# Linear attention's odd units normalised by GpSimd and turned by VectorE through 32x32 squares in memory, even units turned by TensorE

## The chip, the cores and the metric

The kernel runs on one core of a Trainium2 chip. The time is the device time in microseconds (us) of one execution. The engines of the core are TensorE (PE), VectorE (DVE), ScalarE (ACT), GpSimd (POOL) and SyncE (SP), which issues nearly all transfers. They run independently and meet at semaphores.

## What is computed

The input is x of shape (16, 56, 56, 128) in float32. Layer 0 is a group norm and window attention (7x7 windows, shifted by 3), with a residual. Then, with t of shape (16, 3136, 128):

```
t = t + linear_attention(layernorm(t))   # this stage is changed
t = t + recurrence(layernorm(t))

def linear_attention(x):                 # per image, causal
    q, k, v = split(x @ W.T + b)
    q = elu(q) + 1;  k = elu(k) + 1
    num[t] = q[t] @ cumsum(outer(k, v))[t]
    den[t] = q[t] . cumsum(k)[t] + 1e-6
    return num / den

def recurrence(x):                       # batch norm of x @ W.T, then
    y = sigmoid(wx[t] + y @ V.T)         # one step per token
```

## The kernel before

There are three stages in one program: window attention (128 window rows of 392 tokens, pipelined steps n), linear attention, and the scan of the recurrence. The middle one is changed. `pipeline` runs the window stage's steps on each engine and calls the next step of the linear stage inside them from a step `join` on; when the window stage is over, the linear steps run alone. `join` is derived from `JOIN` (125) with an offset for each engine: SyncE `JOIN - 3`, GpSimd `JOIN + 1`, the others `JOIN`.

The linear stage has 196 units of 256 tokens, each two chunks `a` of 128 tokens. Its steps are numbered -4 to 204. Every engine has an order of work written by hand for step n, and each piece waits for semaphores that count units:

- SyncE loads the tokens of unit n+4 into `xc` (L780), and stores finished rows of unit n-5 with their statistics into the table `t2`, in `pieces` that don't cross a 196-token segment (L789). Buffers: 8.
- VectorE measures unit n+3 and the finished unit n-4 (`measure`, L1118, and `aggregate`, L1130), combines queries and keys of unit n (`combine`, L1085), takes denominators, normalises unit n+2 (`normalise`, L1071 for the first four, then L1074), computes the output tokens of unit n-3 (`attend`, L1145) and masks the scores (`inner_out`, L1095).
- GpSimd adds epsilon and takes the root of the variances (`statistics`, L1019 and L1025), and copies 1/std into the table's rows (`remember`, L1030).
- TensorE turns the normalised tokens of unit n+1 (`turn_tokens`, L825) into PSUM, multiplies with the weights (`queries_and_keys`, L835, `values`, L847), turns the keys (L857), forms scores (L870), the outer products (L886), numerators (L904, L908) and second moments (L921).
- ScalarE copies the turned tokens to `uT` and adds 1 (`turned_out`, L951), takes exponentials (L958), evicts values, keys and states, and scales the finished tokens (L993).

The order on TensorE in step n is:

```python
queries_and_keys(n)
turn_keys(n - 1)
turn_tokens(n + 1)
outer(n - 2, 0)
numerators(n - 3)
moments(n - 8)
outer(n - 2, 1)
values(n + 1)
scores(n)
```

In the window stage, the pieces that share the queues with the first linear steps are: GpSimd lowers the scores by their peak (L618), normalises the next unit (L611), weighs the probabilities by 1/sum (L625) and adds the bias to the residual tokens; from `JOIN` on the linear step is run ahead of the weighing. TensorE turns the weighed probabilities (L333). VectorE adds the residual (L455) into `y`, which has four buffers. SyncE loads residual tokens (L223) and stores `y` (L232) to `x1`, from which the linear stage loads.

## Time and profile before

| | us |
|---|---|
| median of 3 runs | 1789.76 (1787.34 to 1792.07) |
| profiled execution | 1784.76 |
| its span in the trace | 1782.8 |
| TensorE busy in the span | 1749.7 |
| VectorE busy | 1509.8 |
| ScalarE busy | 1269.8 |
| GpSimd busy | 1073.7 |

The linear stage's matmuls with the query and key weights start at 771.1 us and end at 1555.5; the window stage lies before, the scan behind. All figures of the profile are from the one profiled execution. Matmul rows overlap each other, so their distance from start to start counts, not their duration. TensorE's granted clock is 1.00 of its full speed in all stages shown but a few microseconds at the seams.

### The profile page before, as it was taken

The numbers are of one execution on the slowest core, as the hardware profiler recorded it, in microseconds if no ns is written. First come the engines' busy times: TensorE is split into PE (matmuls) and PEld (weight loads), VectorE is DVE, ScalarE is ACT, GpSimd is POOL, SyncE is SP. The second block draws the span as 40 slices with busy tenths as digits, with TensorE's granted clock in tenths as the row PEclk, the third lists the DMA queues.
The fourth block names the chain that finished last, engine by engine and source line by source line (L and its number), as shares of the span: only waits on it lengthen the run. The fifth ranks groups of instructions, "written<-read, shape, count | busy, mean of one in ns | idle before, by whom it ended". The sixth has DMA issues, their size and how long they took to land.

```text
span 1782.8 us, 58142 instructions
## 1 busy us (share of the span) xinstructions
PE 1749.7 (98%) x19648; PEld 1587.7 (89%) x19648; DVE 1509.8 (85%) x4546; ACT 1269.8 (71%) x3387; POOL 1073.7 (60%) x1202
## 2 busy tenths in 40 slices
PE   7999999999999999989999999999999999989997
PEld 6888888888888888879999999999999999989997
DVE  7889888888888888778888888888888888868787
ACT  5877778887887788856666666666666666657776
POOL 6887888888888888843333333333333333368874
PEclk9999999999999999999999999999999999999999
DMA  5333343433333332313334434343434443457774
GB/s 167 105 103 104 104 110 99 109 107 102 110 103 104 106 106 70 83 43 70 73 67 68 70 68 70 68 67 68 70 68 70 68 68 70 86 178 277 291 278 176
DMA packets 361816, 188.30 MB, mean 106 GB/s; under 512 B 221760, under 2 KB 348720, under 8 KB 356656
## 3 DMA queue, kind: packets, MB, share of 16 engines
q1 hardware_dynamic: 360368, 183.40, 41.0%
q8 instruction: 164, 2.69, 0.7%
q14 instruction: 132, 1.08, 0.2%
q10 hardware_dynamic: 1152, 1.13, 0.2%
HBM read 106.58 MB, written 77.87 MB: 103 GB/s over the span
## 4 chain that ended last, share of the span: by engine, by line
PE 52%; issue 28%; POOL 17%; DVE 1%; DMA 1%; POOLq 0%; ACT 0%; ACTq 0%; SPq 0%; DVEq 0%
POOL la_rstd L1025 12%; PE k_psum L349 7%; PE k_psum L299 6%; PE k_psum L292 6%; PE k_psum L1488 6%; PE k_psum L317 6%; PE k_psum L333 6%; PE k_psum L365 5%; PE k_psum L1478 5%; PE k_psum L283 5%; POOL la_spread L1019 3%; POOL la_tn L1030 2%; DMA wa_group<-in_group 0%; POOLq L42 0%; DMA t<-la_tn 0%
## 5 line engine op out<-in xcount | busy, mean ns | idle before, releaser
L1019 POOL TENSOR_SCALAR la_spread<-la_mv 128x4 f32<-128x4 f32 (+1 forms) x203 | 46.2, 228 | 476.1 <-DVE la_mv L1130 476.0
L618 POOL TENSOR_TENSOR wa_prob<-wa_prob,wa_peak 128x784 f32<-128x784 f32 x128 | 195.0, 1523 | 116.8 <-DVE wa_peak L484 116.8
L966 ACT ACTIVATE la_ve<-k_psum 128x256 f32<-128x256 f32 x196 | 75.6, 386 | 231.9 <-PE k_psum L847 231.9
L1025 POOL TENSOR_TENSOR la_rstd<-la_spread,k_exponent 128x4 f32<-128x4 f32 (+1 forms) x203 | 207.8, 1024 | 17.2 <-POOL la_spread L1019 0.4
L625 POOL TENSOR_TENSOR wa_prob<-wa_prob,wa_inv 128x784 f32<-128x784 f32 x128 | 195.2, 1525 | 11.3 <-DVE wa_inv L445 11.3
L835 PE MATMUL k_psum<-la_uT,la_wt 128*128 128x256 f32 x784 | 201.9, 380 | 0.0
L1085 DVE SCALAR_TENSOR_TENSOR la_fqk<-k_psum,la_raised 128x512 f32<-128x512 f32 x196 | 135.4, 691 | 72.8 <-ACT la_raised L958 72.6
L1562 ACT ACTIVATE sc_y<-k_psum,sc_cols 128x128 f32<-128x128 f32 x414 | 152.3, 368 | 51.9 <-PE k_psum L1488 8.8
L476 DVE TENSOR_TENSOR wa_prob<-k_psum,wa_bias 128x784 f32<-128x784 f32 x128 | 124.9, 976 | 66.2 <-PE k_psum L317 66.1
L1488 PE MATMUL k_psum<-sc_y,sc_vT 128*128 128x128 f32 x824 | 171.0, 289 | 0.0
L958 ACT ACTIVATE la_raised<-k_psum,la_minus_one 128x512 f32<-128x512 f32 x196 | 134.8, 688 | 43.9 <-PE k_psum L835 43.7
L1478 PE MATMUL k_psum<-sc_uT,sc_fT 128*128 128x128 f32 x832 | 161.7, 276 | 2.8 <-DVE sc_uT L1503 2.8
L525 ACT ACTIVATE wa_kb<-k_psum,wa_own 128x392 f32<-128x392 f32 x256 | 136.5, 584 | 38.2 <-PE k_psum L292 38.2
L544 ACT ACTIVATE wa_vb<-k_psum 49x256 f32<-49x256 f32 x256 | 97.0, 379 | 90.8 <-PE k_psum L299 89.1
L333 PEld LDWEIGHTS k_psum<-k_ident,wa_prob 113*128 113x128 f32 x1024 | 118.2, 142 | 43.5 <-issue 23.7
L886 PE MATMUL k_psum<-la_ve,la_kt 128*128 128x129 f32 (+1 forms) x768 | 150.7, 278 | 1.8 <-ACT la_state L982 1.6
L904 PE MATMUL k_psum<-la_ve,la_aT 128*128 128x129 f32 x784 | 151.7, 276 | 0.0
L908 PE MATMUL k_psum<-la_state,la_fqk 128*128 128x129 f32 (+1 forms) x768 | 148.9, 275 | 0.0
L637 POOL TENSOR_TENSOR wa_xb<-wa_xw,wa_bout 112x384 f32<-112x384 f32 (+1 forms) x128 | 146.9, 1148 | 0.0
L349 PE MATMUL k_psum<-wa_pT,wa_vb 128*64 128x49 f32 x4096 | 146.5, 224 | 0.1
L556 ACT ACTIVATE wa_pT<-k_psum 128x452 f32<-128x452 f32 x256 | 140.2, 548 | 8.4 <-PE k_psum L333 5.3
L349 PEld LDWEIGHTS k_psum<-wa_pT,wa_vb 128*64 128x64 f32 x4096 | 130.0, 138 | 17.8 <-ACT wa_pT L556 0.5
(137 smaller groups left out, 5205.3 us busy)
## 6 DMA issues: line engine op xcount, KB each, us to landing
la_xc<-x SPq DMA_DIRECT2D x196, 128.0 KB, 3.0
wa_xT<-in_x_cm SPq DMA_DIRECT2D x124, 196.0 KB, 3.3
sc_tb<-t SPq DMA_DIRECT2D x17, 1320.0 KB, 8.3
out<-sc_ob SPq DMA_DIRECT2D x17, 1280.0 KB, 5.4
wa_xw<-in_x_tok SPq DMA_DIRECT2D x64, 224.0 KB, 2.7
wa_xw<-in_x_tok SPq DMA_DIRECT2D x64, 168.0 KB, 2.3
x<-wa_y SPq DMA_DIRECT2D x64, 168.0 KB, 2.8
x<-wa_y SPq DMA_DIRECT2D x48, 224.0 KB, 2.9
```

What stands on the lines that cost most here:

```text
L333: mm = nc.tensor.transpose(b_pt[:, q * LANES:(q + 1) * LANES], prob[0:LANES, k % S, hp, 2 * h + p].rearrange("p j c -> p (j c)"), ident[0: ...
L349: mm = nc.tensor.matmul(b_ot[64 * hp:64 * hp + 64, c:c + WIN], vb[:, k % S, h * 2 + w // 2, w % 2, hp].rearrange("p a b -> p (a b)"), pT[: ...
L618: nc.gpsimd.tensor_tensor(s, s, peak[:, k % S, :].unsqueeze(2).broadcast_to([128, PAIRS * HEADS, WIN]), ALU.subtract).then_inc(lowered, 1)
L625: nc.gpsimd.tensor_tensor(s, s, inv[:, k % S, :].unsqueeze(2).broadcast_to([128, PAIRS * HEADS, WIN]), ALU.mult).then_inc(weighted, 1)
L835: mm = nc.tensor.matmul(b_qk[:, j * 2 * P:(j + 1) * 2 * P], wt[:, j * C:(j + 1) * C], uT[:, n % S, :], start=True, stop=True)
L886: nc.tensor.matmul(b_kv[:, 0:E], kt[part, n % S, a, :], ve[part, n % S, a, :], start=fresh, stop=True, skip_group_check=True).then_inc(kv_ ...
L904: mm = nc.tensor.matmul(held[:, a * E:(a + 1) * E], aT[:, n % S, a, :], ve[:, n % S, a, :], start=True, stop=begins(c), skip_group_check=True)
L908: mm = nc.tensor.matmul(held[0:p, a * E:(a + 1) * E], fqk[:, n % S, 0, a * P:a * P + p], state[:, c % S, :], start=False, stop=True, skip_ ...
L1025: nc.gpsimd.tensor_tensor(rstd[:, n % S, used], spread[:, used], exponent[:, used], ALU.pow).then_inc(rooted, 1)
L1478: nc.tensor.matmul(b_state[h][t % 2][:, 0:HALF], ffn.fT[:, :], uT[:, t // 2 % U_PAIRS, t % 2, half(h)], start=True, stop=False).then_inc(w ...
L1488: nc.tensor.matmul(b_state[h][t % 2][:, 0:HALF], ffn.vT[:, :], before, start=False, stop=True).then_inc(v_done[h], 1)
L1562: nc.scalar.activation(ffn.state(t)[:, half(h)], b_state[h][t % 2][:, 0:HALF], ACT.Sigmoid, bias=ffn.shift_bn).then_inc(y_made[h], 1)
```

## The change

Units are treated by parity. Even units go as before, with tiles of their own (`ue`, two buffers). Odd units are normalised by GpSimd (one `tensor_scalar` a chunk, with 1/std and a shift `1 - mean/std` that GpSimd computes, so that the added 1 is in it) into `uo`, which holds two odd units, laid out in quads of 32 channels. Every four units SyncE stores `uo` to the tensor `squares` in memory and loads it back in four pieces into `us`, so that each 32x32 square lies where its transpose is wanted but for the turn inside the square. VectorE turns the squares of one unit with one transpose instruction straight into `uT`. TensorE's turns and ScalarE's eviction remain for even units only.

What moves with it: the loads of tokens run ten units ahead instead of four (14 buffers instead of 8), measuring and roots eight instead of three, `AHEAD` is 12 instead of 7, so that finished units are measured at the same step as before; the linear steps begin at -10 instead of -4 and `JOIN` is `NU - 9` (119) instead of `NU - 3`. The raised values have two buffers instead of four. The table's rows of a chunk are stored with one transfer, without `pieces`.

```diff
-        JOIN = NU - 3
+        JOIN = NU - 9
...
-        XS = 8
-        AHEAD = 7
+        XS = 8
+        XC = 14
+        NS = 10
+        RS = 2
+        AHEAD = 12
...
+        shift = sb("shift", [P, 2])
+        ue = sb("ue", [P, 2, 2, C])
+        uo = sb("uo", [P, QUADS, 4, SQ])
+        us = sb("us", [128, QUADS, 4, SQ])
...
+        def table_rows(c):
+
+            first, block = c * P, SQ * STEPS
+            return bass.AP(t2.tensor, (first % block * NB + first // block) * SF, [[NB * SF, P], [block * NB * SF, QUADS], [1, SF]])
...
-        steps = range(-4, UNITS + 9)
+        def await_tokens(eng, n):
+
+            eng.wait_ge(odd_turned if n % 2 else even_out, n // 2 + 1)
+
+        steps = range(-10, UNITS + 9)
...
+                def store_normed(n):
+
+                    if not inside(n, UNITS) or n % 4 != 3:
+                        return
+                    sp.wait_ge(odd_normed, n // 2 + 1)
+                    sp.dma_start(squares[n // 4], uo[:, :, :, :].rearrange("p q a r -> p q (a r)")).then_inc(uo_stored, 16)
+
+                def load_squares(n):
+
+                    if not inside(n, UNITS) or n % 4 != 1:
+                        return
+                    sp.wait_ge(uo_stored, (n // 4 + 1) * 16)
+                    at_least(sp, odd_turned, n // 2)
+                    for q in range(QUADS):
+                        sp.dma_start(us[q * SQ:(q + 1) * SQ].rearrange("p k a r -> p k (a r)"),
+                                     squares[n // 4, :, q, :].rearrange("(k p) r -> p k r", p=SQ)).then_inc(us_loaded, 16)
...
-                    for a, p, q, col, s in pieces(n):
-                        dst = bass.AP(t2.tensor, ((col % SQ * STEPS + s) * NB + col // SQ) * SF,
-                                      [[NB * SF, q - p], [SQ * STEPS * NB * SF, QUADS], [1, SF]])
-                        sp.dma_start(dst, tn[p:q, n % XS, a]).then_inc(stored[n % XS], 16)
+                    for a in range(2):
+                        sp.dma_start(table_rows(2 * n + a), tn[:, n % XS, a]).then_inc(stored[n % XS], 16)
...
-                    load(n + 4)
+                    load(n + 10)
+                    load_squares(n + 3)
                     store(n - 5)
+                    store_normed(n + 7)
...
                 def turn_tokens(n):
-                    if not inside(n, UNITS):
+
+                    if not inside(n, UNITS) or n % 2:
                         return
...
                 def turned_out(n):
-                    if not inside(n, UNITS):
-                        return
-                    act.wait_ge(u_turned, n + 1)
+                    if not inside(n, UNITS) or n % 2:
+                        return
+                    act.wait_ge(even_turned, n // 2 + 1)
...
+                def place_shift(n):
+
+                    if not inside(n, UNITS) or n % 2 == 0:
+                        return
+                    pool.wait_ge(rooted, n + 1)
+                    at_least(pool, odd_normed, n // 2)
+                    nc.gpsimd.tensor_tensor(shift[:, :], mv[:, n % NS, 0, :, 0], rstd[:, n % NS, 0:2], ALU.mult).then_inc(lowered, 1)
+                    pool.wait_ge(lowered, n // 2 + 1)
+                    nc.gpsimd.tensor_scalar(shift[:, :], shift[:, :], -1.0, 1.0, ALU.mult, ALU.add).then_inc(shifted, 1)
+
+                def normalise(n):
+
+                    if not inside(n, UNITS) or n % 2 == 0:
+                        return
+                    pool.wait_ge(shifted, n // 2 + 1)
+                    at_least(pool, uo_stored, n // 4 * 16)
+                    for a in range(2):
+                        last = nc.gpsimd.tensor_scalar(uo[:, :, n % 4 // 2 * 2 + a, :], quads(xc[:, n % XC, a, :]), rstd[:, n % NS, a:a + 1],
+                                                       shift[:, a:a + 1], ALU.mult, ALU.add)
+                    last.then_inc(odd_normed, 1)
...
-                    statistics(n + 3)
-                    remember(n + 3 - AHEAD)
+                    place_shift(n + 7)
+                    normalise(n + 7)
+                    statistics(n + 8)
+                    remember(n + 8 - AHEAD)
...
+                def turn_tokens(n):
+
+                    if not inside(n, UNITS) or n % 2 == 0:
+                        return
+                    dve.wait_ge(us_loaded, (n // 4 + 1) * 16 * QUADS)
+                    at_least(dve, qk_ready, n - S + 1)
+                    at_least(dve, v_ready, n - S + 1)
+                    nc.vector.transpose(uT[:, n % S, :], us[:, :, n % 4 // 2 * 2:n % 4 // 2 * 2 + 2].rearrange("p k a r -> p a k r")).then_inc(odd_turned, 1)
...
-                    measure(n + 3)
+                    measure(n + 8)
                     combine(n)
                     denominators(n - 3)
                     invert(n - 3)
                     normalise(n + 2)
-                    aggregate(n + 3)
+                    turn_tokens(n + 2)
+                    aggregate(n + 8)
                     attend(n - 3)
                     inner_out(n)
```

## Rows read from the trace of the kernel before

**Rows 1.** Stages: busy us (instructions) of PE, PEld, DVE, ACT, POOL; clock; DMA; GB/s.

```profile
400.00:600.00 200.00, 200.00 (x3117) 167.74 (x3116) 177.44 (x299) 160.20 (x376) 166.47 (x147) 1.00 0.39 106
...
760.00:800.00 40.00, 34.09 (x309) 29.60 (x306) 27.95 (x97) 19.71 (x57) 17.10 (x23) 0.96 0.16 39
...
1100.00:1200.00 100.00, 100.00 (x799) 95.66 (x799) 86.08 (x402) 65.67 (x200) 36.52 (x75) 1.00 0.40 68
```

**Rows 2.** Timeline of TensorE in the linear stage: start us, us, engine, line.

```profile
1101.95 1.03 PE L835 MATMUL k_psum<-la_uT,la_wt 128*128 128x256 f32 x4
...
1103.03 0.38 PE L825 MATMUL k_psum<-k_ident,la_u 128*128 128x128 f32 x2
...
1103.25 0.39 PE L886 MATMUL k_psum<-la_ve,la_kt 128*128 128x129 f32 x2
...
1105.93 1.03 PE L835 MATMUL k_psum<-la_uT,la_wt 128*128 128x256 f32 x4
```

**Rows 3.** Timeline of VectorE and GpSimd in the same stretch.

```profile
1103.73 0.69 DVE L1085 SCALAR_TENSOR_TENSOR la_fqk<-k_psum,la_raised 128x512 f32<-128x512 f32 x1 [0.38 <-ACT la_raised L958]
...
1104.85 0.60 DVE L1074 TENSOR_SCALAR la_u<-la_xc,la_mv,la_rstd 128x128 f32<-128x128 f32 x2
...
1105.65 0.58 DVE L1145 SCALAR_TENSOR_TENSOR la_tn<-k_psum,la_rden,la_xc 128x128 f32<-128x128 f32 x2
...
1105.83 0.23 POOL L1019 TENSOR_SCALAR la_spread<-la_mv 128x4 f32<-128x4 f32 x1 [2.38 <-DVE la_mv L1130]
...
1107.24 0.20 POOL L1030 COPY la_tn<-la_rstd 128x8 f32<-128x8 f32 x1
```

**Rows 4.** Groups from 900 to 1400 us: xcount, busy us, mean ns, idle before.

```profile
L835 PE MATMUL k_psum<-la_uT,la_wt 128*128 128x256 f32 x500 | 128.6, 380 | 0.0
...
L1074 DVE TENSOR_SCALAR la_u<-la_xc,la_mv,la_rstd 128x128 f32<-128x128 f32 x250 | 75.3, 343 | 0.8 <-issue 0.8
...
L825 PE MATMUL k_psum<-k_ident,la_u 128*128 128x128 f32 x250 | 47.7, 273 | 0.0
```

**Rows 5.** Groups of VectorE in the scan, 1580 to 1740 us.

```profile
L1503 DVE STREAM_TRANSPOSE sc_uT<-sc_ub 128x512 f32<-128x512 f32 x84 | 56.5, 672 | 5.4 <-PE k_psum L1478 5.4
```

**Rows 6.** Groups of GpSimd in the window stage, 300 to 600 us.

```profile
L611 POOL TENSOR_SCALAR wa_xn<-wa_xT,wa_rstd,wa_shift 128x392 f32<-128x392 f32 x52 | 35.3, 679 | 0.0
```

**Rows 7.** Timeline of VectorE at the join.

```profile
751.69 0.56 DVE L455 TENSOR_TENSOR wa_y<-k_psum,wa_xb 112x384 f32<-112x384 f32 x1
...
762.45 0.81 DVE L1071 SCALAR_TENSOR_TENSOR la_u<-la_xc,la_mv,la_rstd 128x128 f32<-128x128 f32 x2
...
765.45 2.33 DVE L1071 SCALAR_TENSOR_TENSOR la_u<-la_xc,la_mv,la_rstd 128x128 f32<-128x128 f32 x2
```

**Rows 8.** Timeline of GpSimd at the join.

```profile
745.89 1.53 POOL L625 TENSOR_TENSOR wa_prob<-wa_prob,wa_inv 128x784 f32<-128x784 f32 x1
...
749.68 1.52 POOL L618 TENSOR_TENSOR wa_prob<-wa_prob,wa_peak 128x784 f32<-128x784 f32 x1 [1.30 <-DVE wa_peak L484]
751.19 0.68 POOL L611 TENSOR_SCALAR wa_xn<-wa_xT,wa_rstd,wa_shift 128x392 f32<-128x392 f32 x1
...
766.31 1.32 POOL L637 TENSOR_TENSOR wa_xb<-wa_xw,wa_bout 112x512 f32<-112x512 f32 x1
```

**Rows 9.** Timeline of TensorE at the join.

```profile
749.98 0.55 PE L333 MATMUL k_psum<-k_ident,wa_prob 113*128 113x113 f32 x4
```

**Rows 10.** DMA issues of the page: xcount, KB each, median us to landing.

```profile
la_xc<-x SPq DMA_DIRECT2D x196, 128.0 KB, 3.0
...
x<-wa_y SPq DMA_DIRECT2D x64, 168.0 KB, 2.8
```

**Rows 11.** Timeline of table stores: in the linear stage and at its end.

```profile
1103.48 1.50 SPq L789 DMA_DIRECT2D t<-la_tn  x3
...
1562.89 5.44 SPq L789 DMA_DIRECT2D t<-la_tn  x10
```

**Rows 12.** Waits of VectorE, 1500 to 1580 us: total, times, longest.

```profile
DVE la_stats L1118 <- DMA la_xc<-x: 2.0, 1, 2.0
```

More of the change, by code:

```diff
@@ L69, in build @@
     x1 = nc.dram_tensor("x1", (B, T, C), F32, kind="Internal").ap()
+    squares = nc.dram_tensor("squares", (B * T // 1024, 128, QUADS, 4 * SQ), F32, kind="Internal").ap()
     t2 = nc.dram_tensor("t2", (C, STEPS, NB, SF), F32, kind="Internal").ap()
@@ L85, in build @@
     with ExitStack() as ctx:
-        linear = linear_attention(nc, ctx, x1, t2, attn_wt, attn_b, masks_d, ident, ones, exponent, gram, bank,
+        linear = linear_attention(nc, ctx, x1, squares, t2, attn_wt, attn_b, masks_d, ident, ones, exponent, gram, bank,
                                   ffn, signals, (ffn_w, ffn_wt, ffn_vt, gamma, beta))
@@ L702, in linear_attention @@
         folded = sem("la_folded")
-        loaded = [sem(f"la_loaded{i}") for i in range(XS)]
+        loaded = [sem(f"la_loaded{i}") for i in range(XC)]
+        uo_stored, us_loaded = sem("la_uo_stored"), sem("la_us_loaded")
         stored = [sem(f"la_stored{i}") for i in range(XS)]
@@ L723, in quads @@
             return tile.rearrange("p (q r) -> p q r", q=QUADS)
-        def pieces(n):
-            found = []
-            for a in range(2):
-                first = (2 * n + a) * P
-                token = first
-                while token < first + P:
-                    upto = min(first + P, (token // STEPS + 1) * STEPS)
-                    found.append((a, token - first, upto - first, token // STEPS, token % STEPS))
-                    token = upto
-            return found
+        def table_rows(c):
+            first, block = c * P, SQ * STEPS
+            return bass.AP(t2.tensor, (first % block * NB + first // block) * SF, [[NB * SF, P], [block * NB * SF, QUADS], [1, SF]])
         def stores_through(k, units):
-            return 16 * sum(len(pieces(m)) for m in range(k, units, XS))
+            return 32 * len(range(k, units, XS))
         def quotient_bank(n):
@@ L1116, in measure @@
                             for a in range(2):
-                                tokens = tn[:, m % XS, a, :, 0:SQ] if which else xc[:, m % XS, a, :]
+                                tokens = tn[:, m % XS, a, :, 0:SQ] if which else xc[:, m % XC, a, :]
                                 last = nc.vector.bn_stats(stats[:, n % S, which, a, :], tokens)
@@ L1129, in aggregate @@
                             for a in range(2):
-                                last = nc.vector.bn_aggr(mv[:, n % S, which, a, :], stats[:, n % S, which, a, :])
+                                last = nc.vector.bn_aggr(mv[:, n % NS, which, a, :], stats[:, n % S, which, a, :])
                     last.then_inc(aggregated, 1)
```

89 lines of the change are left out of this document (46 added, 43 removed).

## The prediction

> **What bounds the kernel now.** I read the busy table by stages first. In the linear attention stage TensorE is busy for the whole 100 us that are shown, VectorE for 86, ScalarE for 66 and GpSimd for 37 [rows 1]. A busy TensorE is not yet a bound, so I looked at one period in the timeline: from one start of the query and key matmuls (L835) to the next are 1105.93 - 1101.95 = 3.98 us [rows 2], and no TensorE row in it has idle time before it. The groups of the stage say the same over 500 us: L835 and L825 have 0.0 us of idle time [rows 4]. Each group starts at the fixed distance that its columns give. So TensorE streams without a gap, and this stage is 196 units at about 3.98 us. The chain of waits puts "issue" and GpSimd's root first there; that chain ends behind TensorE and is no bound, since GpSimd sat idle for 2.38 us before the statistics of this very period [rows 3]. What TensorE no longer has to do is therefore gained, as long as nobody else needs more than the new period.
>
> **Terms: what is removed.** Of the 196 units 98 are odd. For each of them TensorE loses its two turns (L825). The group starts at 1103.03 and the next one, L886, at 1103.25 [rows 2]: 0.22 us each, although the rows themselves last 0.27, because they overlap. 98 x 0.22 = 21.6 us. An odd unit's turn is missing in an even step, so the pair of steps falls from 7.96 to 7.74 us. ScalarE loses 98 evictions (L951) and VectorE 98 pairs of normalisations (L1074, 2 x 0.34 us less their overlap) [rows 4]; neither sets the period, so both count nothing by themselves.
>
> **What is added, and what hides it.** VectorE gets one transpose of 128x256 per odd unit. The scan's transpose of 128x512 took 672 ns [rows 5]; half the elements lie between half of that, 0.34 us, and all of it, 0.67. I take 0.42, nearer to the half, as a little of it is fixed. It replaces a pair that takes 0.60 us [rows 3]. VectorE has 86.08/100 x 3.98 = 3.43 us per unit [rows 1], 6.85 a pair, and about 6.67 after the change (6.92 at the upper bound), against 7.74. At least 0.8 us a pair stay free.
>
> GpSimd gets per odd unit two operations of two elements and two normalisations of 128 elements. The nearest rows are 0.20 us for a copy of 8 elements [rows 3] and 679 ns for 392 elements [rows 6]. With the 4-element add at 0.23 us [rows 3] that slopes by about 1.2 ns an element: near 0.37 us for 128, between 0.23 and 0.68. I take 2 x 0.2 + 2 x 0.37 and some 0.15 us of gaps, 1.3 us per odd unit (bounds 1.0 and 1.9). It goes in front of the statistics, into the 2.38 us that GpSimd now waits for VectorE [rows 3], so even 1.9 us doesn't delay the next root. If that cover were gone the root would be late, and then ScalarE's scaled tokens and the table rows behind it.
>
> **The way through memory.** Every four units (two odd ones) SyncE stores one tile of 256 KB (128 x 512 x 4 bytes) and loads it back in four pieces. An issue takes 1.50/3 = 0.5 us in the steady stage [rows 11], and a transfer lands after 2.6 to 3.0 us (rows of 128 and 168 KB, median 3.0 and 2.8) [rows 10]. The stores of table rows become two per unit, where now 640 pieces lie in 392 chunks, 3.3 per unit; with the load that is 4.3 issues a unit before, and 1 + 2 + 5/4 = 4.25 after. SyncE's worst step has seven issues, 3.5 us, still under the period. Are the squares late? SyncE's step m begins at the end of VectorE's attend of step m-1 (L1145 ends at 1106.23) [rows 3]. The loads are issued in 2.4 us and the last lands about 2.8 us after it started, 4.8 to 5.4 us after that point. VectorE turns the unit in its step m+1, at about the place of L1074: 1104.85 + 2 x 3.87 - 1106.23 = 6.4 us after it. A slack of about 1 us, plus about 1 us that TensorE would allow VectorE before its next numerators. I cost this at nothing; if it is eaten, VectorE waits once in four units. Each 1 us beyond the slack would cost 49 us over the stage, so this is the steepest term. The loads of residual tokens get six steps more of lead; a wait of 2.0 us for one of them near the early table loads [rows 12] should go, worth 0.5 us (0 to 2) at TensorE.
>
> **The join with the window stage is where I see a loss.** The first stage is bound by TensorE too (200 of 200 us) [rows 1]; its 52 normalisations in 300 us [rows 6] make 5.8 us a unit. The linear stage's side work now begins six steps earlier there, while first-stage work of all engines still runs.
>
> First, GpSimd. It is busy for 166.47 of 200 us [rows 1], so it has 0.168 x 5.8 = 1.0 us free in a step, before the lowering (L618, 1.30 us in the step shown) [rows 8]. A unit's statistics take 1107.24 - 1105.83 = 1.4 us [rows 3] and an odd unit's normalisation 1.3 more, ahead of the weighing (L625). The window steps concerned are n = 122 to 126, two of them with an odd unit: 5 x 1.4 + 2 x 1.3 - 4 x 1.0 = 5.6 us is the last weighing late. A weighing ends at 745.89 + 1.53 = 747.42 and TensorE turns its result at 749.98 [rows 8, 9], so 2.56 us are covered and some 3 are left.
>
> Second, SyncE's own queue. Its linear steps run four ahead of VectorE's at the join (offset 126 against 129 and 130), and in step -4 it now waits for the odd unit 3, which GpSimd normalises only in window step 126. Behind that wait stand the window stage's loads of tokens (L223) and stores of y (L232). VectorE's sum of unit 122 (L455, at 751.69) [rows 7] needs the store of unit 118 to be complete, because y has four buffers. GpSimd's step 126 begins at 749.68, lowering and normalising end at 751.87 [rows 8], the shift and odd unit 3 at 753.2 or, with the step's start late by 4 x 1.4 + 1.3 - 4.0 = 2.9 us, 756.1. Then come two issues and 2.8 us of landing [rows 10]: 756.8 to 759.7, so VectorE is 5 to 8 us late. Its own gaps (the first stage's VectorE is busy for 177.44 of 200 us, which leaves 0.66 us a step) and the 2.56 us of lead take 2 to 3 of that. The two losses overlap, since GpSimd catches up while VectorE stands. Together I take +4.5 us, about the middle between 0 (all of it falls into gaps) and 9 (3 and 6 us added). Later blocks of the same kind (steps 0 and 4) fall where TensorE has gaps anyway: from 760 to 800 it is busy for 34.1 of 40 us [rows 1].
>
> **End of the stage.** SyncE issues ten table stores in 5.44 us at the end [rows 11], after which the scan's loads follow. With two per unit it issues 8, which saves one or two behind the last root: -0.5 us (0 to -1).
>
> **Sum.** -21.6 + 4.5 - 0.5 - 0.5 = -18.1 us. The profiled execution took 1784.76 us with a span of 1782.8, so 1766.7 and 1764.7 after. The median of the runs lies 5.0 us above the profiled one; on it the sum gives 1789.8 - 18.1 = 1771.7 us.
>
> **Rivals.**
> Port rival (slower): VectorE and GpSimd block each other. For it: the pair L1071 took 0.81 us at 762.45 but 2.33 us at 765.45, up to 767.78, and GpSimd's operation L637 that ran at the time ended at 767.63 [rows 7, 8]. In the new steady stage GpSimd's odd normalisation lies right behind the copy (L1030, 1107.24 + 0.20) [rows 3], so from 1107.4 to about 1108.8, and the even unit's L1074 starts one period after 1104.85, at 1108.83. Against it: GpSimd's pieces are 0.4 us, so one blocked operation loses at most about that, and VectorE has 0.8 to 1.1 us a pair. It decides from 1.1 us a pair on, and turns the sign at 1.3. With two blocked operations of 0.8 us each pair would be 6.67 + 1.6 = 8.27 us, 0.31 above today's 7.96: 98 x 0.31 + 3.5 = +34, 1824 us. I give slower 6 in 100, by this or by late squares. The Trainium skill (SBUF — State Buffer, "Who interferes with whom") states it as a rule: the port pair that the two share is held for the whole instruction by whoever came first, if VectorE's is in a two-port mode or has two inputs in SBUF. By that rule L1074 and GpSimd's new operation exclude each other; the trace agrees, with the 2.33 against 0.81 us.
>
> Saving lost: some other chain gives the period of the even steps, so the 21.6 us don't come. For it only that ScalarE's and VectorE's gaps there are short (0.38 us before L1085) [rows 3]. Against it: those gaps wait for TensorE itself and move with it. 1771.7 + 21.6 = 1793 us, no change that can be measured; half of it lost, 1782. 9 in 100 and 8 in 100.
>
> Expensive join: VectorE's and GpSimd's lateness add up, and the wait at step 0 strikes too: +10 instead of +4.5, and 1777 us or a little more. 12 in 100.
>
> Free join: the lateness falls into gaps that the hand-over has anyway, +0: 1767 us. 15 in 100. That leaves 50 in 100 for the forecast, whose own range is 1768 to 1776 us.
>
> **How the numbers follow.** A measurement of this kernel tells some 0.3% (5.4 us) from no change. The range is 1763 to 1784 us: below, the free join with tail, load wait and 3 us of spread between runs; above, the expensive join with a part of the saving lost. Faster by over 0.3% are the forecast, both joins and half a saving: 0.85. Within 0.3%: 0.09. Slower: 0.06.
>
> **What the profile after will show.** L825 down to half its count, still without idle time, and starts of L835 alternately about 3.76 and 3.98 us apart; TensorE still busy for all of the 100 us. VectorE's transpose near 0.42 us, with no wait for a DMA before it. GpSimd near 53% in this stage. L1074 with a mean above 343 ns if the port is contended. Between 745 and 790 a new wait of TensorE and VectorE, and SyncE waiting for GpSimd's new normalisation with y's stores behind it. What would make me wrong: VectorE waiting for the squares in every fourth step, or a pair of periods above 7.8 us.

## The result, and the profile after

The changed kernel took 1846.27 us (median of 4 runs, 1844.45 to 1850.42) beside 1788.55 us for the kernel before (4 runs, 1784.80 to 1792.07): ratio 1.0326, 95% interval 1.0298 to 1.0355. It is 58 us slower where 18 us faster was forecast. The profiled execution took 1845.93 us, its span is 1844.0 us.

One thing must be known before the experiments. They ran in five later batches, each on one chip (numbers 0, 4, 7, 7 and 5; that of the recorded run is not on record) beside the kernel before on the same chip; there that kernel took 1781.6 to 1782.3 us. In the last three batches, so on two chips, the changed kernel itself ran again, and it took 1769.0 to 1772.1 us. So the change has two results, and both need an explanation. Ratios below are against the kernel before in the same batch.

The page of the changed kernel (busy DMA tenths over 40 slices and moved GB/s; the table stores' queue; the chain by engine and by line; one group; DMA issues with the median time to landing):

```profile
DMA  5333333333333332245589998889989998447774
GB/s 169 103 104 107 107 104 106 103 104 106 107 107 107 101 90 76 76 96 107 104 93 91 88 95 86 89 93 92 94 86 93 91 90 108 103 145 273 284 280 183
...
q1 hardware_dynamic: 393952, 209.10, 59.9%
...
PE 50%; DMA 20%; POOL 16%; issue 12%; DVE 1%; POOLq 1%; ACT 0%; SPq 0%; ACTq 0%; DVEq 0%
DMA squares<-la_uo 19%; PE k_psum L350 7%; POOL la_rstd L1050 7%; PE k_psum L1549 6%; PE k_psum L300 6%; PE k_psum L293 6%; PE k_psum L318 5%; PE k_psum L334 5%; PE k_psum L1539 5%; PE k_psum L366 5%; PE k_psum L284 4%; POOL la_uo L1069 4%;
...
L1069 POOL TENSOR_SCALAR la_uo<-la_xc,la_rstd,la_shift 128x128 f32<-128x128 f32 x196 | 88.4, 458 | 136.6 <-DMA squares<-la_uo 130.0
...
t<-la_tn SPq DMA_DIRECT2D x392, 66.0 KB, 5.0
la_xc<-x SPq DMA_DIRECT2D x196, 128.0 KB, 6.2
...
squares<-la_uo SPq DMA_DIRECT2D x49, 256.0 KB, 9.5
la_us<-squares SPq DMA_DIRECT2D x196, 64.0 KB, 2.3
```

From slice 21 to slice 33 the 16 DMA engines are 80% busy and more and yet move fewer bytes (86 to 95 GB/s) than in slices 18 to 20 (96 to 107). A residual token load of the same 128 KB lands after 6.2 us where it took 3.0 [rows 10]. The store of squares takes 9.5 us, GpSimd waits 130 us for it in all, and it is 19% of the chain.

The stages, with the columns of [rows 1]:

```profile
800.00:900.00 100.00, 99.94 (x787) 94.87 (x786) 87.25 (x405) 62.64 (x193) 53.41 (x130) 1.00 0.50 109
1100.00:1200.00 100.00, 89.46 (x684) 84.18 (x682) 72.46 (x340) 54.15 (x166) 45.61 (x110) 0.98 0.87 88
900.00:1500.00 600.00, 548.34 (x4200) 515.16 (x4199) 451.27 (x2113) 333.34 (x1017) 283.70 (x680) 0.99 0.91 92
```

The first 100 us are the forecast come true: TensorE full, GpSimd at 53%, DMA at half. The rest is another machine: TensorE has lost 52 of 600 us, with the same program. Its granted clock is 0.98 and more in these stretches, so the loss is idle time and not the clock. The waits from 900 to 1400 us (total us, times, longest) name what ends the idle time. In the kernel before the only wait for a transfer there is VectorE's for tokens, 3.3 us in all:

```profile
POOL la_uo L1069 <- DMA squares<-la_uo: 97.3, 28, 5.4
DVE la_uT L1134 <- DMA la_us<-squares: 48.3, 24, 3.1
DVE la_stats L1176 <- DMA la_xc<-x: 43.4, 42, 3.0
...
PE k_psum L928 <- DVE la_aT L1153: 28.1, 18, 2.4
```

One such wait, in the timelines of SyncE and GpSimd (start us, us; idle before it in brackets):

```profile
1192.08 0.38 SPq L792 DMA_DIRECT2D squares<-la_uo  x1
...
1193.91 3.34 SPq L809 DMA_DIRECT2D t<-la_tn  x2
...
1202.36 0.88 POOL L1069 TENSOR_SCALAR la_uo<-la_xc,la_rstd,la_shift 128x128 f32<-128x128 f32 x2 [4.34 <-DMA squares<-la_uo]
```

The store is issued at 1192.08 and lands 10.1 us later. `uo` has one buffer, so GpSimd may not normalise the next odd unit before 1202.2, and the statistics of the following units stand behind that wait. SyncE's two table stores, usually 1.0 us, take 3.34 us to issue here.

**Accounting.** From the first to the last start of the query and key matmuls, and with what lies around them (us; starts from the timeline of TensorE, the last column is the span less the last start):

```
                                first start   last start   between   behind
before                             771.12       1554.84     783.72    227.96
after                              778.74       1616.16     837.42    227.84
changed kernel, e9 (experiment 6)  778.67       1541.45     762.78    228.25
```

After against before: +7.6 at the join, +53.7 in the stage, -0.1 behind it, together +61.2 us, which is 1844.0 - 1782.8. The third row is the same program as the second: same join, but -20.9 us in the stage.

### The profile page after: what moved, and what is told of

It reads as the page before. It is cut to its first block, busy times and chain, and to the rows that moved or that the text cites. A ratio compares the mean times of both kernels' runs of the same rounds, so it can differ in the third digit from the quotient of the medians.

```text
span 1844.0 us, 58387 instructions
## 1 busy us (share of the span) xinstructions
PE 1751.3 (95%) x19452; PEld 1578.2 (86%) x19452; DVE 1487.7 (81%) x4448; ACT 1235.9 (67%) x3289; POOL 1199.4 (65%) x1604
## 4 chain that ended last, share of the span: by engine, by line
PE 50%; DMA 20%; POOL 16%; issue 12%; DVE 1%; POOLq 1%; ACT 0%; SPq 0%; ACTq 0%; DVEq 0%
DMA squares<-la_uo 19%; PE k_psum L350 7%; POOL la_rstd L1050 7%; PE k_psum L1549 6%; PE k_psum L300 6%; PE k_psum L293 6%; PE k_psum L318 5%; PE k_psum L334 5%; PE k_psum L1539 5%; PE k_psum L366 5%; PE k_psum L284 4%; POOL la_uo L1069 4%; POOL la_spread L1043 2%; POOL la_tn L1076 1%; POOL la_shift L1060 1%
## 5 line engine op out<-in xcount | busy, mean ns | idle before, releaser
L1050 POOL TENSOR_TENSOR la_rstd<-la_spread,k_exponent 128x4 f32<-128x4 f32 (+1 forms) x208 | 212.1, 1020 | 17.6 <-POOL la_spread L1043 0.4
L928 PE MATMUL k_psum<-la_ve,la_aT 128*128 128x129 f32 x784 | 155.4, 281 | 47.9 <-DVE la_aT L1153 35.9
L1069 POOL TENSOR_SCALAR la_uo<-la_xc,la_rstd,la_shift 128x128 f32<-128x128 f32 x196 | 88.4, 458 | 136.6 <-DMA squares<-la_uo 130.0
L928 PEld LDWEIGHTS k_psum<-la_ve,la_aT 128*128 128x128 f32 x784 | 119.3, 193 | 54.7 <-issue 44.8
L334 PE MATMUL k_psum<-k_ident,wa_prob 113*128 113x113 f32 x1024 | 143.3, 262 | 4.4 <-POOL wa_prob L626 4.4
```

Of the source, the lines that this page charges most:

```text
L334: mm = nc.tensor.transpose(b_pt[:, q * LANES:(q + 1) * LANES], prob[0:LANES, k % S, hp, 2 * h + p].rearrange("p j c -> p (j c)"), ident[0: ...
L928: mm = nc.tensor.matmul(held[:, a * E:(a + 1) * E], aT[:, n % S, a, :], ve[:, n % S, a, :], start=True, stop=begins(c), skip_group_check=True)
L1050: nc.gpsimd.tensor_tensor(rstd[:, n % NS, used], spread[:, used], exponent[:, used], ALU.pow).then_inc(rooted, 1)
L1069: last = nc.gpsimd.tensor_scalar(uo[:, :, n % 4 // 2 * 2 + a, :], quads(xc[:, n % XC, a, :]), rstd[:, n % NS, a:a + 1], shift[:, a:a + 1], ...
```

## Experiments

Each quoted expectation defines its own letters; the same letter can mean another theory in a later batch. The theories in words: the late squares as such; the traffic of the squares; the merging of the table stores; the alignment of the table rows; SyncE's early join; the memory at hand.

**1. Is it the traffic or the wait?** The kernel before, plus a store of 256 KB in every fourth unit that nobody waits for before the end of the stage (constant content, not the squares, and not read back; `raised`, `bias` and `fold` laid out as in the change, to make room).

```diff
+                def store_normed(n):
+                    ...
+                    sp.dma_start(squares[n // 4], uo[:, :, :, :].rearrange("p q a r -> p q (a r)")).then_inc(uo_stored, 16)
```

> The kernel before, plus one transfer of 256 KB from the core to memory every four units (the store of squares alone, of a constant tile, for which nobody waits; two tiles share memory to make room, and the raised values have two buffers). Theory M (the memory side of the writes is overrun: the 132-byte table rows of the middle blocks begin and end inside a 32-byte piece of memory, and the squares' writes come on top): from about 900 us on the table packets grow from a mean of 14 ns to 25 or more, the DMA share from 0.40 to 0.7 or more, and the 256 KB land after 6 to 10 us; little of it in the time, 1785 to 1800 us, since nobody waits. Rival V (it takes the whole added traffic, loads too): share near 0.45, landing 2.5 to 3.5 us throughout. Rival T (it is the merged table stores, which this kernel hasn't): the same as V.

Measured: 1785.31 us, ratio 1.0018 (1.0008 to 1.0028), DMA share .50 and TensorE 598.11 of 600 us from 900 to 1500; the store lands after 4.5 us, the token load after 3.4. The late landing and the DMA share of 0.7 that theory M expected did not come. Another 256 KB slow all transfers somewhat, but by themselves cost 3.8 us, next to nothing beside the loss. A loss of that size needs someone who waits.

**2. Merged table stores.** The changed kernel with the stores of the kernel before (3.3 per unit instead of 2), and the other way round, the kernel before with merged stores. The first ran in two batches.

```diff
-                    for a in range(2):
-                        sp.dma_start(table_rows(2 * n + a), tn[:, n % XS, a]).then_inc(stored[n % XS], 16)
+                    for a, p, q, col, s in pieces(n):
+                        ...
+                        sp.dma_start(dst, tn[p:q, n % XS, a]).then_inc(stored[n % XS], 16)
```

> The changed kernel with the table rows stored in pieces again, as before. Rival T (the merged stores are what slows the transfers): DMA share back to about 0.5 in the whole linear stage and 1770 to 1785 us. Theories M and V: no help, share still 0.85 or more after 900 us, 1840 to 1860 us; more issues on SyncE make it if anything a little longer.

> The kernel before, with the table rows of a chunk stored by one transfer (392 instead of 640 transfers), nothing else. After the second experiment merging is a suspect of its own: with pieces the changed kernel lost 48 us less. Theory M (the memory takes only so many unaligned rows, and pieces slow their issue): table packets a little slower than 14 ns in the middle blocks, la_xc landing 3.5 to 5 us, time 1780 to 1800 us. Rival T (merged stores alone do it, without squares): table packets of 25 ns and more, share 0.6 or more, 1800 us or more. Without any effect of merging: 14 ns, share 0.40, same time.

> The table stores back in pieces (3.3 a unit instead of 2), in the same batch. Theory M (the merged stores make the pile-up): below the changed kernel by some 45 us. Theory C: the pieces cost issues on SyncE's queue and help nothing, so this run is 15 to 30 us above the changed kernel, which is itself at 1768 to 1780 us.

Measured: 1798.85 us (1.0096, 1.0076 to 1.0116; two runs) in the first batch, and 1770.67 us (0.9930, 0.9913 to 0.9946) in a later one, where the changed kernel took 1771.54. The kernel before with merged stores: 1783.58 us, 1.0006 (0.9996 to 1.0015). After the first batch I took the 47 us between 1798.85 and 1846.27 as the price of merging. That was wrong: side by side on one chip the two don't differ. But the same kernel differs by 28 us between two batches (chips 0 and 7), while the kernel before took 1781.55 us in the one and 1781.68 us in the other. So the time of the kernel before doesn't tell how the transfers of the changed kernel will fare. From 900 to 1500 us, first batch, then the later one (columns of [rows 1]):

```profile
900.00:1500.00 600.00, 579.94 (x4548) 550.63 (x4548) 493.72 (x2294) 359.40 (x1100) 308.33 (x736) 1.00 0.71 99
```

```profile
900.00:1500.00 600.00, 600.00 (x4768) 573.13 (x4767) 520.14 (x2404) 375.18 (x1152) 320.54 (x773) 1.00 0.59 104
```

**3. Alignment of the table rows.** What is odd in the trace after is when the trouble begins, near 905 us. Table rows of 132 bytes lie eight to a token, block b at byte 132 b of 1,056. Only block 0 begins, and only block 7 ends, at a multiple of 32 bytes. A block is 24.5 units, and the stores lag by five, so block 1 begins at unit 29.5, near 900 us. The mean duration of one packet, computed from the trace's packet records (ns):

```
                      800-900 us (block 0)                  950-1500 us (blocks 1 to 7)
                      table row   512 B reads   2 KB pieces   table row   512 B reads   2 KB pieces
before                   14.2        30.0           -            14.5        39.0           -
after                    13.7        32.1          89            34.1        51.2          296
e9, same program         13.7        30.8          89            22.1        39.2          232
e3, padded rows          14.2        28.6          89            14.2        28.1           88
```

The sign was there in the kernel before: reads take 39.0 instead of 30.0 ns once block 0 is done, while its own unaligned rows stay at 14.5. Two tests. First the changed kernel with rows of 160 bytes (28 bytes of zeros more, 21% more table bytes), in three batches, and the kernel before with the same padding:

```diff
+ST = 40
-    t2 = nc.dram_tensor("t2", (C, STEPS, NB, SF), F32, kind="Internal").ap()
+    t2 = nc.dram_tensor("t2", (C, STEPS, NB, ST), F32, kind="Internal").ap()
...
-        tn = sb("tn", [P, XS, 2, QUADS, SF])
+        tn = sb("tn", [P, XS, 2, QUADS, ST])
```

> The changed kernel with table rows of 160 bytes instead of 132 (40 floats, the last seven zero), in memory and in the core, so that each row begins and ends on a multiple of 32 bytes. 21% more bytes in the table. Theory M in its form about unaligned rows: table packets at 14 to 20 ns in all blocks, share near 0.5, squares land in 3 us, linear stage about 758 us, and 1775 to 1790 us with the scan's larger loads. If only volume counts (V): no better than the changed kernel, 1845 to 1870 us.

> The changed kernel with the padded table, in the same batch. If unaligned rows are the condition for the slow transfers, it gives 1763 to 1768 us and squares landing at 2.0 us whatever the changed kernel does beside it.

> The changed kernel with the padded table beside it: 1763 to 1770 us in either case, if the unaligned rows are the condition. If it is slow where the changed kernel is slow, the slow memory alone is enough and alignment is not the cause of the difference.

> The kernel before with the padded table alone (rows of 160 bytes for 132, each a multiple of 32), nothing else of the change. If the alignment only matters through the squares, this is the kernel before within 0.3%, with table and token transfers landing at 2.2 instead of 3.4 and 2.9 us. If the late squares were not all of it, and transfers in the kernel before held something up too, it is 3 to 6 us faster. The scan reads 21% more bytes, which could cost 1 to 3 us at its end.

Measured: 1766.15 us (0.9913, 0.9897 to 0.9930), 1766.49 (0.9913) and 1766.36 us (0.9910). The first of these ran beside the 1798.85 us of experiment 2, so on a chip where unaligned rows cost the change dearly, the aligned ones cost nothing (that run also stored in pieces, which on chip 7 made no difference). Windows and DMA issues from 900 to 1500 us:

```profile
900.00:1500.00 600.00, 600.00 (x4766) 573.23 (x4766) 519.84 (x2405) 375.88 (x1151) 321.77 (x773) 1.00 0.47 111
```

```profile
t<-la_tn SPq DMA_DIRECT2D x310, 80.0 KB, 2.3
la_xc<-x SPq DMA_DIRECT2D x154, 128.0 KB, 2.2
squares<-la_uo SPq DMA_DIRECT2D x39, 256.0 KB, 2.0
```

More bytes (111 instead of 92 GB/s), half the DMA share, and every transfer lands in 2.0 to 2.3 us. The kernel before with padding gains nothing: 1781.29 us, 0.9997 (0.9987 to 1.0007), although its token loads land in 2.1 instead of 3.1 us. Nobody there waits for them.

Second, the same 132-byte rows with the whole table moved by 16 bytes. Now block 3 ends and block 4 begins at a multiple of 32 (132 x 4 + 16 = 544):

```diff
+    wide = nc.dram_tensor("t2", (C * STEPS * NB * SF + 8,), F32, kind="Internal").ap()
+    t2 = wide[4:4 + C * STEPS * NB * SF].rearrange("(c s b f) -> c s b f", c=C, s=STEPS, b=NB)
```

> The changed kernel with the whole table moved by 16 bytes in memory, nothing else. A row of block b then begins at 16 + 4b in a 32-byte piece of memory and ends at 16 + 4(b+1): only block 3 ends and only block 4 begins on a multiple of 32 bytes, where in the changed kernel these were blocks 7 and 0. Theory M about alignment: slow packets (25 ns and more) from the first table stores at about 800 us on, fast ones (14 to 18 ns, share near 0.5) while blocks 3 and 4 are stored (units 74 to 122, about from step 79 to 128), and slow again to the end of the stage. If it is something that builds up with time or with the address of the squares: fast to 900 us and slow to 1570, as in the changed kernel.

Measured: 1773.16 us (0.9950, 0.9930 to 0.9969). Three stretches of the windows, and the squares' time to landing in the same three:

```profile
900.00:1060.00 160.00, 160.00 (x1271) 152.65 (x1271) 138.41 (x639) 100.20 (x308) 85.74 (x205) 1.00 0.55 105
1110.00:1240.00 130.00, 130.00 (x1031) 123.84 (x1030) 112.23 (x521) 80.67 (x247) 68.72 (x165) 1.00 0.47 104
1290.00:1440.00 150.00, 150.00 (x1189) 142.96 (x1188) 129.89 (x602) 94.18 (x289) 80.54 (x193) 1.00 0.55 104
```

```profile
squares<-la_uo SPq DMA_DIRECT2D x10, 256.0 KB, 4.0
```

```profile
squares<-la_uo SPq DMA_DIRECT2D x9, 256.0 KB, 2.1
```

The fast stretch has moved to blocks 3 and 4, and only there does the store land in 2.1 us; in 800 to 900 us, the fast stretch of the changed kernel, the median is now 5.9 us (2.5 there). Nothing but the address of the rows has changed.

**4. SyncE's early join.** SyncE enters the linear stage at the window step of GpSimd instead of four steps earlier, so it doesn't stand before an odd unit that GpSimd has yet to reach. Once alone, once with padding, once again beside the changed kernel.

```diff
-..., following=linear["sync"](sp, await_image), join=JOIN - 3, ...
+..., following=linear["sync"](sp, await_image), join=JOIN + 1, ...
```

> The changed kernel, with SyncE's linear steps begun four window steps later (offset JOIN + 1 instead of JOIN - 3), so that its wait for GpSimd's first odd units no longer stands before the window stage's loads and stores. My account of the join: the 6.2 us wait of VectorE for the store of y goes, the first query and key matmul starts 3 to 6 us earlier (778.7 in the changed kernel), and the time falls by as much or less, since the transfers still bound the stage behind: 1836 to 1846 us. If the join's loss were GpSimd's load alone: the first matmul stays at 778 us.

> Both: rows of 160 bytes and SyncE's later join. From e3_padfull (1766 us, against 1781.5 for before on that chip) minus 3 to 6 us: 1760 to 1764 us, ratio 0.987 to 0.990. If the join's loss is GpSimd's alone: as e3_padfull, ratio 0.991.

> SyncE's late join once more, in the same batch as the changed kernel, so that the two differ in the join alone. Under R: 1762 to 1766 us and some 80 us below the changed kernel. Under C: 1762 to 1766 us where transfers land near 4 us, and 4 to 8 us below the changed kernel, the price of SyncE's wait at the join; where the changed kernel is slow (over 1830 us) this one is slow too (over 1820 us).

Measured: 1763.67 us (0.9898), with padding 1761.45 us (0.9885, 0.9869 to 0.9902), and in the batch of the changed kernel 1764.35 us (0.9908, 0.9887 to 0.9930) beside its 1771.54. The first unit starts at 773.12 instead of 778.67 us. That is worth 5.6 us; the two times of that batch lie 7.2 us apart, of which the traces give 1.7 to the stage (761.06 instead of 762.78 us). The first of the three was over 70 us better than I expected because transfers were faster in its batch (squares after 3.9 us), not because of the join. A row of the page's DMA issues for the padded version:

```profile
squares<-la_uo SPq DMA_DIRECT2D x49, 256.0 KB, 2.0
```

**5. Without the way through memory.** Sixteen copies from SBUF to SBUF per four units in place of one store and four loads (with two buffers for `us`).

```diff
+                    for k in range(QUADS):
+                        for q in range(QUADS):
+                            sp.dma_start(us[q * SQ:(q + 1) * SQ, n // 4 % 2, k]..., uo[k * SQ:(k + 1) * SQ, q]...)
```

> The changed kernel without the way through memory: sixteen transfers of 32 partitions x 512 bytes every four units, from uo straight into us (two buffers), instead of one store and four loads. SyncE issues 28 transfers in four units instead of 17, 12 us of 15.5. Theories M and V: the share stays near 0.5, VectorE no longer waits for squares, the linear stage's steps average 3.87 to 3.95 us, and the time is 1772 to 1790 us. If the wait for the squares were not the cause, 1830 us or more; if SyncE's queue becomes the bound, a pair of steps of more than 8 us, and SyncE without waits.

Measured: 2046.59 us, 1.1476 (1.1453 to 1.1498). SyncE's queue is the bound; from 900 to 1500 us it waits for other engines in only 21 of 600 us, and TensorE's granted clock, with its long idle times, is 0.91 there:

```profile
1105.39 13.31 SPq L795 DMA_DIRECT2D la_us<-la_uo  x16
```

Sixteen issues take 13.31 us, 0.83 us each, and with the other three per unit there is no room in 15.5 us. This says what an issue costs; on memory it says little, as the queue hides it.

**6. The changed kernel again, and a dose.** Unchanged in three batches; and with one more store per unit to a scratch place, 1,024 rows of 132 bytes (unaligned; 264 bytes apart, so that by the same arithmetic every fourth of them does begin on a multiple of 32) or of 128 bytes (aligned, the last number left out).

```diff
+                    sp.dma_start(extra[n % XS, :, :, 0:33], tn[:, n % XS, :, :, 0:33].rearrange("p a q f -> p (a q) f")).then_inc(stored[n % XS], 16)
```

> The changed kernel once more, beside the kernel before on this chip. It tells two readings of the runs so far apart. Theory R (a state of the kernel's own): SyncE's early join puts its queue out of step with the other engines, transfers then land at 9.5 us and stay there; the kernel gives 1840 to 1850 us wherever it runs, and squares land at 9 to 10 us from 950 us on. Theory C (the memory of the chip at hand): unaligned table rows slow the transfers everywhere, but how far differs with the chip; the kernel before took 1788.55 us beside the changed kernel and 1781.6 to 1782.3 us in the two batches since. Then this run, where the kernel before is near 1782, gives 1768 to 1780 us, squares landing near 4 us, and 4 to 8 us more than the kernel with SyncE's late join.

> The changed kernel a third time. If the memory at hand sets it, its time goes with that of the kernel before: near 1770 us where that is near 1782, near 1845 us where that is near 1789, and between where it is between. Squares landing accordingly at 4, 9.5 or between.

> The changed kernel a fourth time: 1769 to 1777 us where the kernel before is near 1782, as in the two batches before; 1840 us or more only where that is near 1789 us too.

> The changed kernel with one more store per unit, which writes the same 1,024 table rows of 132 bytes to a scratch place, 264 bytes apart: twice the unaligned rows. If these rows are what slows the transfers, DMA share goes from about .73 to .9 or more, squares land at 8 us or later, VectorE and GpSimd wait for them in most periods, and the kernel takes 1820 to 1900 us even on a chip where the changed kernel takes 1772. If they are not, the extra issue (0.5 us of SyncE a unit) and the extra packets cost what they cost in the next run.

> The same extra store with rows of 128 bytes, 256 bytes apart (each begins and ends on a multiple of 32 bytes; a table row without its last number): as many packets and issues as in the run before. If alignment matters and not the count of packets, squares land about as in the changed kernel (within 1 us) and the kernel takes 1770 to 1785 us; if the count of small packets or SyncE's issues matter, it is as slow as the run before.

Measured: 1771.54 us (0.9933, 0.9917 to 0.9950), 1772.05 us (0.9947, 0.9908 to 0.9985; 1769.06 to 1777.17) and 1769.00 us (0.9930, 0.9914 to 0.9945). Windows and two waits of the first of them:

```profile
900.00:1500.00 600.00, 598.95 (x4747) 571.32 (x4747) 517.98 (x2394) 374.40 (x1148) 320.03 (x769) 1.00 0.73 104
```

```profile
POOL la_uo L1069 <- DMA squares<-la_uo: 28.6, 22, 2.7
...
DVE la_uT L1134 <- DMA la_us<-squares: 6.6, 7, 1.1
```

The waits are there here too, but 28.6 and 6.6 us instead of 97.3 and 48.3, and GpSimd's and VectorE's free time takes them. From 950 to 1500 us the squares land after 5.3 us (second) and 8.0 us (third), TensorE has lost 1.7 and 5.2 of 600 us; in the recorded run 9.9 us and 52. In the first (e9) the loads that wait for the squares start 7.3 us (median) after the store's issue, so it lands no later.

The slowness also comes and goes inside one run. Two stretches of the second repeat (e13, chip 7), both with unaligned rows:

```profile
1000.00:1180.00 180.00, 180.00 (x1428) 171.84 (x1427) 156.05 (x724) 112.93 (x347) 96.22 (x232) 1.00 0.59 105
1200.00:1320.00 120.00, 119.92 (x950) 114.11 (x949) 103.03 (x478) 74.12 (x228) 63.39 (x155) 1.00 0.85 102
```

The squares land after 5.1 us in the first stretch and 8.2 us in the second, and a table row's packet takes 15.4 and 28.7 ns; after 1340 us it is back at 4.6 us and 15.9 ns. So the same program on the same chip has both conditions, and a chip's number alone doesn't explain them. With the whole table aligned, neither shows in any of the five traces.

The dose ran beside the second. Unaligned: 2172.35 us (1.2190). Aligned: 1807.82 us (1.0145, 1.0096 to 1.0193). Windows and DMA issues, unaligned first:

```profile
900.00:1500.00 600.00, 455.93 (x3023) 419.76 (x3022) 324.49 (x1524) 241.57 (x731) 204.75 (x491) 0.89 1.09 89
```

```profile
squares<-la_uo SPq DMA_DIRECT2D x49, 256.0 KB, 11.0
```

```profile
900.00:1500.00 600.00, 573.55 (x4448) 543.80 (x4448) 481.91 (x2245) 351.28 (x1077) 300.71 (x721) 0.99 0.95 128
```

```profile
squares<-la_uo SPq DMA_DIRECT2D x49, 256.0 KB, 6.2
```

The same number of packets and issues, 3% fewer bytes in the dose, and 365 us less. A part of the unaligned dose's price is TensorE's clock, granted at 0.89 there against 0.99. The aligned dose isn't free, as I had expected (1770 to 1785): 36 us over its base. The table's own unaligned rows go on in it, and a fuller queue makes the squares later; its own 128-byte rows take 22.5 ns a packet there.

## Why the prediction was wrong, and where it was right

**The step that failed** is in the way through memory: "A slack of about 1 us ... I cost this at nothing; if it is eaten, VectorE waits once in four units." The same paragraph called it the steepest term. Its size was 0; it measured +75.3 us in the recorded run (+53.7 in the stage, with 21.6 saved by TensorE) and about +0.7 in the trace of e9. Three things were wrong in it.

First, "a transfer lands after 2.6 to 3.0 us" was taken as a constant (the rows that it names have 2.8 and 3.0). It was a median over a stage in which it already depended on the table rows, and it rose with the traffic that the change itself added: 2.0 us with aligned rows, 4 to 10 us without.

Second, the slack that I worked out is that of the loads. The dearer wait is GpSimd's for its single buffer `uo`: 97.3 us against 48.3. Two units (7.74 us) after the second odd unit's normalisation began it wants to write again; less 0.9 us for the operation itself, 6.8 us remain for SyncE's turn and the landing. The traces of the changed kernel fit: at 5.3 and 8.0 us TensorE loses 1.7 and 5.2 of 600 us, at 9.9 it loses 52, and with the late join and 4.0 us nothing. The landing isn't all of it, though: the version with pieces loses 20 us at 7.0 (experiment 2) and the aligned dose 26 us at 6.2. Both give SyncE more issues a unit, which also takes from the 6.8 us; how much wasn't separated.

Third, the loss isn't 49 us per us over the slack. By that rule 9.9 against 6.8 us would have cost 152 us, twice what was measured. Part of each wait falls into GpSimd's and VectorE's free time, and three kinds of waits (squares stored, squares loaded, tokens) overlap; the runs don't separate their shares.

**The rival that came in** is half of the port rival: "I give slower 6 in 100, by this or by late squares". Late squares stood there without a time of their own, and "VectorE waiting for the squares in every fourth step" in the last paragraph. The port half fell. The Trainium skill (SBUF — State Buffer, "Who interferes with whom") gives the rule, but the trace doesn't bear it out for this pair: even tokens' L1123 takes 345 ns, against 343 [rows 4]. Of its 26 rows from 800 to 900 us 12 overlap a row of GpSimd's L1069, and these take 347 ns, the others 343. Groups of the changed kernel from 800 to 900 us:

```profile
L1123 DVE TENSOR_SCALAR la_ue<-la_xc,la_mv,la_rstd 128x128 f32<-128x128 f32 x26 | 7.9, 345 | 0.0
...
L1134 DVE STREAM_TRANSPOSE la_uT<-la_us 128x256 f32<-128x256 f32 x13 | 5.8, 445 | 0.0
```

**TensorE's saving**, -21.6 us: right. Starts in the undisturbed stretch lie 3.77 and 3.98 us apart (forecast 3.76 and 3.98), and over the stage e9 gives -20.9 us (with padded rows it is -23.2, from 783.7 to 760.5):

```profile
851.87 1.03 PE L859 MATMUL k_psum<-la_uT,la_wt 128*128 128x256 f32 x4
...
855.64 1.03 PE L859 MATMUL k_psum<-la_uT,la_wt 128*128 128x256 f32 x4
...
859.62 0.60 PE L859 MATMUL k_psum<-la_uT,la_wt 128*128 128x256 f32 x2
```

**VectorE's transpose**, 0.42 us: 0.445 measured. **GpSimd**, near 53%: 53.41%; its odd unit takes 1.46 us from the first row's start to the last row's end (853.18 to 854.64), where 1.3 was taken.

**The join**, +4.5 us: the mechanism as written, the size too small, +7.6 us. SyncE's and VectorE's timelines:

```profile
724.50 0.49 SPq L785 DMA_DIRECT2D la_xc<-x  x1
753.80 0.34 SPq L792 DMA_DIRECT2D squares<-la_uo  x1
...
754.66 0.45 SPq L233 DMA_DIRECT2D x<-wa_y  x1
```

```profile
757.69 0.56 DVE L456 TENSOR_TENSOR wa_y<-k_psum,wa_xb 112x384 f32<-112x384 f32 x1 [6.24 <-DMA x<-wa_y]
```

SyncE stands from 725 to 753.80 before odd unit 3, y's store goes out only then, and VectorE stands for 6.24 us (5 to 8 forecast). I had let 2 to 3 us of this fall into gaps; the late join of experiment 4 gets 5.6 of the 7.6 back. The first of the two losses was also read too small: 1107.24 - 1105.83 = 1.4 us runs to the start of the last statistics row, which lasts 0.20 us more, so five units add 1.0 us to the 5.6. **Tail and token wait**, -0.5 us each: not seen. What lies behind the last unit is 227.8 to 228.3 us in all three rows of the accounting.

**The agreement of the absolute times is luck.** The three later batches gave 1771.5, 1772.1 and 1769.0 us beside 1771.7 forecast, but the forecast started from 1789.8 us and the kernel before took 1781.7 to 1781.9 us there. The saving was 10.1, 9.9 and 12.9 us, not 18.1; with transfers that keep their time (padded rows) it was 15.4 to 15.5 us. Most of what was missing seems to lie at the join: three variants of the kernel before (merged stores; padding alone; the store of experiment 1) start their first unit at 767.55, 767.99 and 769.94 us in later batches, the changed kernel at 776.7 to 778.7, so that against them the join costs 7 to 11 us, not 4.5. They are variants, with one trace each, so this is a reading and no test. The sum left out the condition on which its sign hung, and even where that condition held it was some 3 us too good.

**What is shown and what stays open.** Shown: late squares make the loss (waits and chain); whether they are late hangs on the alignment of the table rows (padding, shift by 16 bytes, dose); the same unaligned kernel gives up to 28 us more in one batch than in another, while the padded one stays within 0.4 us on three chips. Not shown: why the recorded run's transfers were slower than those of every later batch. It may be the chip, but batch and chip changed together, and the slowness also changes inside a run (experiment 6). The kernel before was slower beside the recorded run too, by 7 us, but it doesn't follow the others in general (experiment 2). No later batch had transfers that slow, so that the padded version would also hold there is likely, from the pair of experiments 2 and 3 in one batch, but wasn't seen. The best version, padded rows and SyncE's late join, took 1761.45 us, 1.15% less than the kernel before.

## What to carry to other kernels

A transfer's time to landing isn't a constant of its size: before a wait is hung on a DMA, read how landing and packet times vary over the stage, and leave slack for three times the median, as here 9.9 us came of a median of 3.0. A second buffer for `uo` would be the other way; no run tried it. Make rows in memory begin and end on multiples of 32 bytes even when nobody waits for them yet; the cost appears when somebody does. And a change whose gain hangs on a transfer that is just in time can win in one batch and lose in another, so it wants runs in several, on several chips.

## What the runs showed of the hardware

Stores of rows that neither begin nor end on a multiple of 32 bytes slow the core's other transfers: 512-byte reads took 51 ns in the recorded run and 28 with padded rows, 2 KB pieces 296 and 88 ns. Their own packets are slowed only in part of the runs: 34 ns in the recorded run, 14.5 in the kernel before, 15.4 and 28.7 in two stretches of one run (e13). While rows of 132 bytes with one end on a multiple are stored, they take 14 ns and the 2 KB pieces 89, as with rows of 160 bytes and both ends. The Trainium skill (DMA: Bandwidth & Descriptors, "Specifications") says that transfers below 512 bytes lead to a read-modify-write; the runs here differ, as rows of 160 bytes and of 132 bytes with one such end, all below 512, go through without the slowing. Its page Collectives: The Full Stack ("Rules for kernel authors") asks for buffers aligned to 32 bytes for the same reason; that the alignment matters for plain stores too, the shift by 16 bytes bears out. That it is a read-modify-write that takes the time is not shown by any run.

Busy DMA engines aren't fast ones: 87% busy moved 88 GB/s (after, 1100 to 1200 us), 47% busy moved 111 (padded rows).

An issue on SyncE's queue took 0.34 to 0.53 us for tiles of 128 partitions, 0.83 us for copies of 32 partitions from SBUF to SBUF, and up to 1.7 us where the transfers were behind.
